# Edge loop of a two-layer GNN kernel: both one-hots of a group by one VectorE operation, squares in bf16

## The reference, cut to what matters

```python
# x: 1250 nodes x 512; src, dst, edge_weight: 41250 edges, sorted by dst
h = relu(layernorm(x))
# layer 0: message of an edge from both its ends, summed at src
m = relu(concat(h[src], h[dst]) @ W0.T + b0)
x = x + segment_sum(m, src, 1250)
h = relu(layernorm(x))
# layer 1: weighted neighbours, summed at dst, leaky with alpha
g = h @ W1.T
out = segment_sum(g[src] * edge_weight[:, None], dst, 1250)
x = x + where(out >= 0, out, alpha * out)
```

## Time and profile before

| | us |
|---|---|
| median of three runs (1100.72 to 1104.4) | 1104.0 |
| profiled execution | 1098.75 |
| its span, first to last instruction | 1097.1 |

### The profile page before, as it was taken

One profiled execution on the slowest core, in us unless ns is written; L12 is line 12 of the kernel. 1 busy time (PEld: TensorE's weight loads), 2 busy tenths in 40 slices (PEclk: granted clock), 3 DMA queues, 4 the chain that ended last, 5 costly groups with the idle time before them and its releaser, 6 DMA issues. The chain is left out here.

```text
span 1097.1 us, 22493 instructions
## 1 busy us (share of the span) xinstructions
PE 1016.5 (93%) x4835; PEld 805.1 (73%) x4836; DVE 950.8 (87%) x1782; ACT 832.2 (76%) x1751; POOL 737.8 (67%) x1056
## 2 busy tenths in 40 slices
PE   4698999999399999999999999999999999959997
PEld 3376776677278888888887777888878878848775
DVE  7898889896379999999999999999999999973454
ACT  6787677788288888888888888888888888845210
POOL 3888788888557777777777777777777777740000
PEclk8599999999689999999999999999999999989999
DMA  7000000000111111111111111111111111010011
GB/s 206 2 3 3 2 3 2 3 2 3 33 56 41 44 39 44 41 42 42 42 42 42 42 41 43 38 45 39 44 40 44 41 42 42 28 39 1 15 37 43
DMA packets 37957, 38.43 MB, mean 35 GB/s; under 512 B 6448, under 2 KB 34139, under 8 KB 37920
## 3 DMA queue, kind: packets, MB, share of 16 engines
q1 hardware_dynamic: 32772, 37.32, 11.0%
q0 software_dynamic: 4864, 0.33, 1.7%
q10 hardware_dynamic: 284, 0.33, 0.1%
HBM read 34.29 MB, written 3.37 MB: 34 GB/s over the span
## 5 line engine op out<-in xcount | busy, mean ns | idle before, releaser
L1053 ACT ACTIVATE msg_hi<-edge_ps 128x512 fp32r<-128x512 f32 x432 | 257.7, 597 | 81.0 <-PE edge_ps L984 81.0
L914 POOL TENSOR_TENSOR M<-M,pair_w 125x125 f32 x432 | 210.9, 488 | 160.0 <-DVE pair_w L1111 120.5
L1125 DVE SCALAR_TENSOR_TENSOR msg_lo<-edge_ps,msg_hi 128x512 fp32r<-128x512 f32 x432 | 290.6, 683 | 22.3 <-ACT msg_hi L1053 17.5
L370 POOL DMA_INDIRECT edge_table<-fields,row_no x150 | 196.5, 1310 | 45.8 <-issue 45.8
L898 POOL TENSOR_TENSOR hot_w<-hot_d,weight_l 128x252 fp32r<-128x252 bf16 x216 | 181.7, 841 | 0.0
L978 PE MATMUL edge_ps<-b_hi,turned_d 125*128 x432 | 172.9, 400 | 7.1 <-ACT turned_d L1037 6.4
L727 ACT ACTIVATE lane_piece<-hot_lane,fields 125x128 fp32r<-125x128 bf16 x480 | 151.4, 392 | 35.7 <-DVE hot_lane L450 35.0
L939 PE MATMUL node_ps<-msg_hi,hot_s 128*125 128x512 f32 x432 | 176.2, 408 | 0.2 <-DVE msg_lo L1125 0.2
L983 PE MATMUL edge_ps<-a_hi,turned_s 125*128 x432 | 171.1, 396 | 0.3 <-ACT turned_s L1037 0.3
L979 PE MATMUL edge_ps<-b_lo,turned_d 125*128 x432 | 171.1, 396 | 0.0
L984 PE MATMUL edge_ps<-a_lo,turned_s 125*128 x432 | 170.8, 395 | 0.0
(11 more groups left out here) (207 smaller groups left out, 1712.9 us busy)
## 6 DMA issues: line engine op xcount, KB each, us to landing
spread<-edge_rows SPq DMA_DIRECT2D x216, 125.0 KB
out_dram<-result SPq DMA_DIRECT2D x10, 250.0 KB
edge_table<-fields,row_no POOLq DMA_INDIRECT x150
w_in<-in_L_gnn_W_dram SPq DMA_DIRECT2D x1, 2048.0 KB, 12.5
S<-in_x_dram SPq DMA_DIRECT2D x1, 1792.0 KB
w_in<-in_L_gnn_W_dram SPq DMA_DIRECT2D x1, 1024.0 KB, 5.2
S<-in_x_dram SPq DMA_DIRECT2D x1, 448.0 KB
edge_table<-zeros SPq DMA_DIRECT2D x1, 432.0 KB, 15.4
```

The source lines that it names most:

```text
L370: pool.indirect_dma_start(table_dram[:, :], bass.IndirectOffsetOnAxis(ap=row_no[:, c:c + 1], axis=0), fields[:, c, 0:TABLE_FIELDS], None). ...
L914: pool.tensor_tensor(part, part, pair_w[h][:, j, 0, 0:BN], ALU.add).then_inc(m_added, 1)
L1053: act.activation(msg_hi[j][:], edge_ps[j][:], ACT.Relu).then_inc(hi_ready, 1)
L1125: dve.scalar_tensor_tensor(out=msg_lo[j][:], in0=edge_ps[j][:], scalar=0.0, in1=msg_hi[j][:].bitcast(F32), op0=ALU.max, op1=ALU.subtract). ...
```

## The change

Three things are changed in the edge loop. local_d and local_s become two halves of one tensor local_ds, and hot_d and hot_s of a group two halves of one fp32r tensor hots, so that one is_equal of 2 x 4 x 126 = 1008 elements writes both. This instruction stands behind the fourth residual, with both waits ahead of it; hot_d was made behind the third. hot_d is now fp32r instead of bf16, and GpSimd reads it as f32. The tile square is bf16 instead of f32. Outside the loop the unused ident_b and its copy on ScalarE go, and neg_mean moves to the first stage's memory.

```diff
@@ buffers @@
-        ident_b = sb("ident_b", [P, P], BF16)
...
-        local_s = sb("local_s", [P, NT], F32)
-        local_d = sb("local_d", [P, NT], F32)
+        local_ds = sb("local_ds", [P, 2, NT], F32)
+        local_d, local_s = local_ds[:, 0, :], local_ds[:, 1, :]
...
-                    act.copy(ident_b[:], ident[:])
...
-        hot_s = [sb(f"hot_s{k}", [P, GRP, OHW], F32R, scope) for k in range(2)]
-        hot_d = [sb(f"hot_d{k}", [P, GRP, OHW], BF16, scope) for k in range(2)]
+        hots = [sb(f"hots{k}", [P, 2, GRP, OHW], F32R, scope) for k in range(2)]
+        hot_d, hot_s = ([pair[:, f] for pair in hots] for f in range(2))
...
-        square = sb("square", [BN, GRP * P], F32, scope)
+        square = sb("square", [BN, GRP * P], BF16, scope)
@@ GpSimd @@
-                        pool.tensor_tensor(hot_w[h][:, :, f, :], hot_d[k][:, h * PAIR:(h + 1) * PAIR, :],
+                        pool.tensor_tensor(hot_w[h][:, :, f, :], hot_d[k][:, h * PAIR:(h + 1) * PAIR, :].bitcast(F32),
@@ VectorE @@
-                def make_hots(hot, local, g):
-
-                    return dve.tensor_tensor(hot[:], iota[:, 1:1 + OHW].unsqueeze(1).to_broadcast([P, GRP, OHW]),
-                                             local[:, bass.ds(g * GRP, GRP)].unsqueeze(2).to_broadcast([P, GRP, OHW]),
-                                             ALU.is_equal)
+                def make_hots(k, g):
+
+                    shape = [P, 2, GRP, OHW]
+                    dve.tensor_tensor(hots[k][:], iota[:, 1:1 + OHW].unsqueeze(1).unsqueeze(1).to_broadcast(shape),
+                                      local_ds[:, :, bass.ds(g * GRP, GRP)].unsqueeze(3).to_broadcast(shape),
+                                      ALU.is_equal).then_inc(hots_d, 1)
...
-                        if j == 2 and not last:
-                            if start != 0:
-
-                                dve.wait_ge(hots_w, g * 4)
-                            make_hots(hot_d[1 - k], local_d, g + 1).then_inc(hots_d, 1)
                         if j == 3:
                             if not last:
                                 if start != 0:
 
+                                    dve.wait_ge(hots_w, g * 4)
                                     dve.wait_ge(m_ready, g * 2)
-                                make_hots(hot_s[1 - k], local_s, g + 1)
+                                make_hots(1 - k, g + 1)
...
-                make_hots(hot_d[0], local_d, 0).then_inc(hots_d, 1)
-                make_hots(hot_s[0], local_s, 0)
+                make_hots(0, 0)
```

More of the change, by code:

```diff
@@ L104, in build @@
         eps_t = sb("eps_t", [P, 1], F32)
-        neg_mean = sb("neg_mean", [P, NBLK], F32)
         rstd = sb("rstd", [P, NBLK], F32)
@@ L200, in build @@
             sums = sb1("sums", [BN, 3, NBLK], F32)
+            neg_mean = sb1("neg_mean", [P, NBLK], F32)
             psum = scope.enter_context(nc.psum_tensor("psum1", [P, 8, 512], F32))
@@ L576, in _ @@
                     own(dve.tensor_tensor(code[:], raw[:, :, CODE_AT], code_ps, ALU.add))
[L577 to L581, removed]
+                    own(dve.tensor_scalar(local_d, code[:].bitcast(I32), 1.0 / 65536.0, None, ALU.mult))
+                    own(dve.tensor_scalar(local_s, local_d, -(TILE - 1) / 2, 1.0 / TILE, ALU.add, ALU.mult))
+                    own(dve.tensor_scalar(local_s, local_s, MAGIC, None, ALU.add))
+                    own(dve.tensor_scalar(local_s, local_s, -MAGIC, None, ALU.add))
+                    own(dve.scalar_tensor_tensor(out=local_d, in0=local_s, scalar=-float(TILE), in1=local_d,
                                                  op0=ALU.mult, op1=ALU.add))
-                    own(dve.tensor_scalar(local_s[:], local_s[:], -float(SHIFT_S - 1), 0.0, ALU.add, ALU.max))
+                    own(dve.tensor_scalar(local_s, local_s, -float(SHIFT_S - 1), 0.0, ALU.add, ALU.max))
                 @block.tensor
```

## The result

| | before | after |
|---|---|---|
| median of the runs, us | 1103.7 (1100.72 to 1104.4) | 1116.67 (1112.82 to 1118.48) |
| profiled execution, us | 1098.75 | 1118.23 |
| its span, us | 1097.1 | 1116.4 |
| first to last msg_hi of the edge loop, us | 305.67 to 967.29 | 308.29 to 986.59 |
| period of a group, us | 6.140 | 6.297 |

The changed kernel is slower by 1.2%: the ratio of after to before is 1.0118, with the interval 1.0083 to 1.0153. The forecast of 1111 us had the sign right and about half of the size: 7 us in place of 13. Of the 19.3 us by which the span grew, 16.7 lie in the edge loop (678.30 against 661.62 us) and 2.6 ahead of it.

The account below looks back on a forecast made before the run. TensorE was taken to bound the kernel at 6.14 us a group; after the change VectorE and GpSimd's mutual holds give about 6.205, 0.065 more in about 100 groups: +6.5 on 1104.0, 1111 us. Its own range was 1107.5 to 1120, overall 1100 to 1122.

Parts of the forecast that it names:

- What bounds the kernel before: Edge loop: TensorE issues back to back and sets the pace, 6.11 us of slots in a 6.14 us group period.
- (a): VectorE: two one-hot operations become one of 1008 elements, 1.10 us against 1.18; 0.08 us less a group, worth nothing.
- Rival 3: VectorE sets the pace after all; each group gives back up to 0.10 us, 1093 us; chance 0.10.
- (b): Destination one-hot moves past the fourth residual; the next group's first residual comes 0.51 us later, more than its room.
- The step that watched the first residual: Group's first residual comes 0.51 us later against 0.26 + 0.19 of room, so its node product waits for msg_lo.
- rival 2: Combined operation ahead of hot_w_l holds it 0.51 us longer; TensorE's weight product waits; +17, 1121 us; chance 0.13.
- The period of 6.20: Expected sign in the profile after: an edge-loop group period of 6.20 us; staying at 6.14 would refute the prediction.
- (c): VectorE's wait on hots_w moves behind the fourth residual, after the awaited hot_w has ended; costs nothing.
- (d): GpSimd reads hot_d as f32: 0 to 0.08 us more per hot_w, 0.04 taken; dearer end gives 1118 us.
- (e): ScalarE's tile square written in bf16: 720 against 722 ns, so the type costs nothing.
- The sum: VectorE and GpSimd links per group add to about 6.205 us against TensorE's 6.14; +6.5 us, 1111 us.
- the ring: Way through VectorE and GpSimd from one combined operation to the next sets the period, about 6.205 us; chance 0.42.

Follow-up runs that it names:

- e1: Changed kernel with the one-hots again as two operations at their old places, new types kept: 1098.24 us, ratio 0.9968 to the kernel before.
- e9: Changed kernel with two one-hots at their old places, new types, and TensorE's weight product behind tile 2's edge products: 1097.61 us, ratio 0.9982 to before.
- e2: Changed kernel with the one-hots as two operations of 504 elements, both behind the fourth residual: 1141.64 us, ratio 1.034 to before.
- e3: Changed kernel with GpSimd making the next group's first-pair hot_w ahead of the two adds into M: 1132.44 us, ratio 1.027 to before.
- e8: Changed kernel with TensorE's first-pair weight product moved behind the next group's first-tile node product: 1120.76 us, ratio 1.0189 to before.
- e10: Changed kernel with VectorE's join ahead of the S add at the first pair only: 1131.11 us, ratio 1.0325 to before.
- e11: Changed kernel with VectorE's joins ahead of their S adds at both pairs: 1113.84 us, ratio 1.0167 to before.
- e7: Changed kernel with TensorE's first-pair weight product one tile of edge products later, behind tile 2's: 1112.86 us, ratio 1.0132 to before.
- e5: Changed kernel with ScalarE's copy of pair_w ahead of the square behind a group's first msg_hi: 1117.1 us, ratio 1.0136 to before.
- e12: Changed kernel with the first tile's residual on VectorE, between the two joins, cut into four of 128 columns: 1135.49 us, ratio 1.0374 to before.
- e13: Changed kernel with the third tile's residual on VectorE, ahead of the fourth, cut into four of 128 columns: 1112.73 us, ratio 1.0146 to before.

## Why the prediction was right, and what was mis-sized

**What bounds the kernel before.** Right: e1 and e9 go at 6.125 and 6.117 and about the time of before, near the 6.11 of TensorE's slots, and every kernel in which TensorE lost clearly more time to waits is slower.

**(a), the combined operation.** 1.10 was 1.12 where free, and it was held only once, for 0.15 us in the mean. Rival 3, faster, fell: the operation count is lower in after, and it is slower than e1 by 0.172 us a group. But the saving of merging is real beside e2. It just couldn't pay for the place.

**(b), the place.** Right: e1 and e2 put the cost here. The step that watched the first residual was wrong in its sign, though. I expected node products of a group's first tile to wait for msg_lo; in after none do, and the room in front of them is never under 0.32 us, where it was 0.31 at the least before. TensorE waited for hot_w_l at the place of rival 2 instead, which the prediction itself had named as a sign of being wrong. The period of 6.20 that it had named as a sign of being right came out as 6.297. The expected waits did appear in e2, e3, e8, e10 and e11, where the orders of the two engines are others.

**(c), the wait on hots_w.** Nothing in after points to it: for the operation at 610.02 the last hot_w of the group before was done at 607.97 + 0.78 = 608.75.

**(d), the f32 operand.** 0.04 was the middle of 0 and 0.08; it is 0: 609 ns with f32 and with bf16. The Trainium skill, GPSIMD Engine Reference, section "Performance versus the Vector engine", gives one rate for two-input operations and says nothing of a narrower operand being cheaper; the prediction had read the dearer end and 1118 us out of it. That this is near the time that came is an accident, since the term measured zero.

**(e), the square.** Right, 718 against 720 ns, and no part of e1's time.

**The sum.** Each link, as the prediction had it and as the mean of some 96 groups of after:

| link | predicted | after |
|---|---|---|
| hot_w to the first join (0.48 + 1.10 + 0.59) | 2.17 | 0.331 + 1.862 = 2.193 |
| first join to the next group's first join | 2.13 | 2.133 |
| join to M add (0.83 and 1.05) | 0.94 | 0.900 |
| M add to the second (0.63 and 0.58) | 0.605 | 0.611 |
| second M add to hot_w | 0.36 | 0.459 |
| sum | 6.205 | 6.296 |

A sum of distances round a loop equals the period whether or not it is critical, so that the right column gives 6.297 proves nothing. What makes it a cause are the constant 0.48 in 84 groups, the period that stayed when TensorE's wait was moved (e7), and, with the limit told above, the dose. What the table does show is the mis-sized term: 0.09 is missing in all, and the last link alone is 0.10 too short. I took it from one pair of rows, 608.52 to 608.88, which lies within a group. The link of the ring goes over the end of a group, and GpSimd's loop runs over two groups, so every second time it turns there: 609.30 to 609.66 is 0.36, 615.62 to 616.16 is 0.54 in the rows of after above. With 0.45 in its place, the mean of these two, the sum would have been 6.295, and by the prediction's own count 0.155 x 100 = 15.5 us, or 1119.5.

6.297 less 6.140 gives 16.8 us over the loop, and the medians differ by 13.0: the profiled execution of before was 5 us below its median, that of after 1.6 above. The 2.6 us in the first stage are within what the profiled executions differ by (the first msg_hi comes between 302.82 and 310.42 us in the fourteen of them), and no run here separates them.

**The chances.** The ring and rival 2 were kept apart, with prices of 7 and 17 us, and the truth has a piece of each: the ring's period, shown at rival 2's place. e7 says that the second is the symptom. There was luck in the number: the measured 1116.67 lies in the ring's own range of 1107.5 to 1120 only because its upper bound took in a price for the f32 operand (0.16 us a group) that measured zero, while the link that was really longer had no range at all.

## What to carry to other kernels

When one operation of an engine is made from two, ask first where the longer one will stand, then what it saves: here the merging was worth 0.22 us a group and the place cost 0.39. If two engines hold each other up, add up the way round through both, with each link read where the ring passes, over a loop's turn too, and compare the sum with the bound's slots. And before a wait that TensorE shows is treated as the cause, take it away: if the period stays (e7), it was the symptom; if the time only takes another name (e5), the name was wrong. A fixed dose inside and outside the suspected way (e12, e13) tells more than a rearrangement, which makes collisions of its own (e3, e10, e11), but look there too whether the groups still follow each other as before.

## What the runs showed of the hardware

- VectorE and GpSimd alternated at operations with two SBUF inputs: in all 96 groups of after the queued combined operation went between two hot_w, 0.48 to 0.50 us after the start of the first. A combined operation of 1008 elements was held once, by at most 0.42 us; two of 504 at the same place were held twice, 1.73 us for the pair in the mean. GpSimd's hot_w_l, 0.61 us free, is recorded as 1.57 us behind it, 0.96 more. A VectorE add with one operand in PSUM took 0.59 us beside a running hot_w, as alone.
- A GpSimd multiply of 252 elements takes 609 ns with a bf16 and with an f32 operand, beside a broadcast one.
- After a wait TensorE's next slots were longer: 618.43 to 618.75, 0.32 us, for two matmuls of half a slot each, which take 0.235 elsewhere. Such restarts cost up to 0.10 us each in after (0.11 in e2), 4.6 us in all behind its weight products.
